# The recurrence scan written out, with key times value as a third rank-one term of VectorE's update

## What is computed

```python
def step(S, inp):
    qt, kt, vt, at, gft = inp
    bs1 = jnp.einsum('bhk,bhkv->bhv', kt, S)
    S1 = S + at[..., :, None] * bs1[..., None, :]
    S2 = jnp.exp(gft)[..., None] * S1
    bs2 = jnp.einsum('bhk,bhkv->bhv', kt, S2)
    S3 = S2 + at[..., :, None] * bs2[..., None, :] + kt[..., :, None] * vt[..., None, :]
    o = jnp.einsum('bhk,bhkv->bhv', qt, S3)
    return (S3, o)
```

## Time and profile before

| what | value |
|---|---|
| median of 3 runs (lowest, highest) | 6515.56 us (6512.77, 6517.51) |
| the profiled execution, its own time | 6517.93 us |
| its span, first to last instruction | 6516.2 us |
| VectorE busy over the span | 3547.5 us (54%) |
| TensorE busy over the span | 5086.6 us (78%) |
| ScalarE, GpSimd busy over the span | 2825.8 us, 1792.3 us |
| VectorE's chief group in the layers, L1878 | idle ahead of it 452.0 us, 441.1 of it until TensorE's L1067 |

### The profile page before, as it was taken

How to read it: one execution, slowest core, us unless ns; L and a number is a source line. 1 busy time by engine, 2 the same in 40 slices (tenths; PEclk the granted TensorE clock), 3 DMA queues, 4 the chain that set the end, 5 groups by cost and what they waited for, 6 DMA issues and landing times. The chain is left out here.

```text
span 6516.2 us, 116951 instructions
## 1 busy us (share of the span) xinstructions
PE 5086.6 (78%) x37588; PEld 3128.5 (48%) x37588; DVE 3547.5 (54%) x15640; ACT 2825.8 (43%) x5416; POOL 1792.3 (28%) x3788
## 2 busy tenths in 40 slices
PE   7998999999999999969989989991000003998999
PEld 5775555555555555557744447760000002444676
DVE  2225666666666666522246631227888886664111
ACT  3334666666666666523335533331000000553333
POOL 1012556555565655510112210000111110221000
PEclk9998999999999999979989979995555555998999
DMA  1000000000000000000010000001000000000000
GB/s 50 1 0 9 2 2 9 2 9 2 9 2 5 6 5 2 1 1 1 0 27 2 2 3 1 0 19 71 0 0 0 0 0 11 2 2 1 1 0 13
DMA packets 36317, 43.85 MB, mean 7 GB/s; under 512 B 15584, under 2 KB 23040, under 8 KB 35456
## 3 DMA queue, kind: packets, MB, share of 16 engines
q1 hardware_dynamic: 35840, 37.74, 1.9%
HBM read 27.64 MB, written 10.09 MB: 6 GB/s over the span
## 5 line engine op out<-in xcount | busy, mean ns | idle before, releaser
L1398 PEld LDWEIGHTS ps<-w,arena 128*128 128x128 f32 x8192 | 1071.4, 192 | 463.0 <-issue 458.9
L1878 DVE CUSTOM_DVE_ANT_0 arena<-ps,mask_win 128x256 f32<-128x256 f32 (+1 forms) x3072 | 1011.2, 386 | 452.0 <-PE ps L1067 441.1
L1728 ACT ACTIVATE arena<-ps,eb 128x512 f32<-128x512 f32 x1024 | 703.6, 687 | 1120.3 <-PE ps L1388 1120.3
L2097 DVE SCALAR_TENSOR_TENSOR X<-ps,C,X 128x128 f32 (+1 forms) x1024 | 289.1, 344 | 1474.1 <-PE ps L1398 1473.1
L1398 PE MATMUL ps<-w,arena 128*128 128x128 f32 x8192 | 1083.6, 275 | 0.0
L1388 PE MATMUL ps<-arena,w 128*128 128x512 f32 x2048 | 1055.2, 598 | 4.6 <-ACT arena L1722 4.6
L1563 ACT ACTIVATE arena<-ps 128x512 f32<-128x512 f32 (+1 forms) x1536 | 754.4, 544 | 598.6 <-PE ps L1077 596.8
L1077 PE MATMUL ps<-arena 32*128 32x512 f32 (+1 forms) x3072 | 873.2, 589 | 16.6 <-ACT arena L1563 10.1
L1067 PE MATMUL ps<-arena 32*128 32x256 f32 (+1 forms) x6144 | 834.0, 381 | 39.8 <-ACT arena L1536 38.6
L1491 PE MATMUL ps<-arena,ones 128*128 128x342 f32 x16 | 9.4, 764 | 967.6 <-DVE arena L2315 964.2
L1067 PEld LDWEIGHTS ps<-arena 32*128 32x128 f32 x6144 | 494.8, 185 | 324.4 <-issue 102.6
(11 more groups left out here) (260 smaller groups left out, 7856.5 us busy)
## 6 DMA issues: line engine op xcount, KB each, us to landing
w<-in_L_w_dram SPq DMA_DIRECT2D x2, 2048.0 KB
scr_k<-arena SPq DMA_DIRECT2D x8, 256.0 KB, 2.1
scr_v<-arena SPq DMA_DIRECT2D x8, 256.0 KB, 2.3
scr_f<-arena SPq DMA_DIRECT2D x8, 256.0 KB, 2.3
arena<-scr_k SPq DMA_DIRECT2D x1, 2048.0 KB, 7.9
arena<-scr_f SPq DMA_DIRECT2D x1, 2048.0 KB, 12.4
arena<-scr_v SPq DMA_DIRECT2D x1, 2048.0 KB, 16.8
out_dram<-X SPq DMA_DIRECT2D x1, 2048.0 KB, 8.7
```

The source lines that it names most:

```text
L1398: m = pe.matmul(ps[:, 2 + (p * E + e) % 2, i * P:(i + 1) * P], hid[c % 2][:, i * P:(i + 1) * P], W2(e)[:, c, :], start=(c == 0 and i == 0) ...
L1728: act.activation(hid[c % 2], ps[:, c % 2, :], gelu, bias=b1(e)[:, c:c + 1])\
L1878: x = dve.tensor_tensor_reduce(out=seen, in0=bank[:, s.at(v):s.at(v) + s.kw], in1=mask, scale=1.0, scalar=NO_SCORE, op0=ALU.add, op1=ALU.m ...
```

## The change

Five things change together:

- The loop over turns of 8 steps becomes 512 steps written out one after the other. All values that are waited for are constants; the register instructions, branches and gates are gone.
- GpSimd's product and the semaphore `kv_ready` are gone. L2292 with them: the decayed state goes straight into column 0 of MJ. In its place the outer product has three terms: k times v, a times w.S, u times k.S.
- MJ has rows of four floats, for three before.
- The four vectors of a step, (w, k, a, u), lie in one array KU, and VectorE reads them from there: the first multiply takes rows 0 and 1, the outer product rows 1 to 3. ScalarE copies the value v beside the two dot products (VXY) and the decay (Fs), and no longer copies KW and UA.
- The loaded keys lie in TMP and their squares in SQ, where they were in UA and TMP.

```diff
-        KW = take(TOKENS, 2, HD)
-        UA = take(TOKENS, 2, HD)
+        KU = take(TOKENS, 4, HD)
...
-        KV = take(STEP_RING, HD, HD)
-        FS = take(HD, HD)
-        MJ = take(HD * HD, 3)
+        MJ = take(HD * HD, 4)
...
-        XY = take(2, HD)
+        VXY = take(STEP_RING, 3, HD)
...
-            with pool.Fori(0, TOKENS // STEP_RING) as it:
...
-                    pool.tensor_tensor(slot, vv, kk, ALU.mult).then_inc(R.kv_ready, 1)
...
-            with act.Fori(0, TOKENS // STEP_RING) as it:
...
-                    act.activation(KWs[:, ring], KW[:, bass.ds(t0, half)], copy)
-                    act.activation(UAs[:, ring], UA[:, bass.ds(t0, half)], copy)
...
+            for h in range(TOKENS // half):
+
+                act.wait_ge(R.step, half * h + 1)
+                times = slice(half * h, half * (h + 1))
+                ring = slice(half * (h % 2), half * (h % 2 + 1))
+                act.activation(VXY[:, ring, 0, :], VD[:, :, times].rearrange("p v t -> p t v"), copy)
+                act.activation(Fs[:, ring], FD[:, :, times].rearrange("p k t -> p t k"), copy)\
+                    .then_inc(R.staged, 1)
...
-            kn, wv, ua, av = KW[:, :, 0, :], KW[:, :, 1, :], UA[:, :, 0, :], UA[:, :, 1, :]
-            chain.link(dve.tensor_tensor(TMP, KD, KD, ALU.mult))
+            wv, kn, av, ua = (KU[:, :, r, :] for r in range(4))
+            chain.link(dve.tensor_tensor(SQ, KD, KD, ALU.mult))
...
+            for t in range(TOKENS):
+                j = t % STEP_RING
+                s = SH[:, (j - 1) % STEP_RING]
+                new = SH[:, j]
+                if t % half == 0:
+                    dve.wait_ge(R.staged, t // half + 1)
+                dve.wait_ge(R.step, t + 1 + half)
+                chain.add(dve.tensor_tensor(
+                    M1.rearrange("p (r v) k -> p r v k", r=2),
+                    s.unsqueeze(1).broadcast_to([P, 2, HD, HD]),
+                    KU[:, t, 0:2, :].unsqueeze(2).broadcast_to([P, 2, HD, HD]), ALU.mult))
+                chain.add(dve.tensor_tensor(
+                    MJ[:, :, 0].rearrange("p (v k) -> p v k", k=HD), s,
+                    Fs[:, j].unsqueeze(1).broadcast_to([P, HD, HD]), ALU.mult))
+                dve.wait_ge(v_chain, chain.value() - 1)
+                chain.link(dve.tensor_reduce(VXY[:, j, 1:3, :].rearrange("p r v -> p (r v)"), M1, AX_X, ALU.add))
+                chain.link(dve.tensor_tensor(
+                    MJ[:, :, 1:4].rearrange("p (v k) r -> p r v k", k=HD),
+                    KU[:, t, 1:4, :].unsqueeze(2).broadcast_to([P, 3, HD, HD]),
+                    VXY[:, j].unsqueeze(3).broadcast_to([P, 3, HD, HD]), ALU.mult))
+                dve.tensor_reduce(new.rearrange("p v k -> p (v k)"), MJ, AX_X, ALU.add).then_inc(R.step, 1)
+                if t >= TOKENS - SEEN and j == STEP_RING - 1:
+
+                    seen = slice(t - (TOKENS - SEEN) - j, t - (TOKENS - SEEN) + 1)
+                    dve.wait_ge(R.step, t + 2 + half)
...
```

More of the change, by code:

```diff
@@ L49 @@
 ROOT_AT = (1, 1)
-PER_TURN = {'dve causal': (26, 2), 'pool causal': (26, 2), 'scan': (40,), 'scan seen': (42,),
+PER_TURN = {'dve causal': (26, 2), 'pool causal': (26, 2),
             'pool moe 2': (52, 4), 'pool moe 1': (26, 2), 'dve moe input': (38, 4),
@@ L335, in __init__ @@
         self.scan_in = sem("r_scan_in")
-        self.kv_ready = sem("r_kv_ready")
         self.staged = sem("r_staged")
@@ L478, in build @@
         GATE = take(BATCHES, OUT)
-        KD = UA.rearrange("p a b c -> p (a b c)")[:, 0:HD * TOKENS].rearrange("p (a b) -> p a b", b=TOKENS)
+        KD = TMP
+        SQ = KU.rearrange("p a b c -> p (a b c)")[:, 0:HD * TOKENS].rearrange("p (a b) -> p a b", b=TOKENS)
         at[0] = 4 * HD * TOKENS + 2 * HD * TOKENS
-        KV = take(STEP_RING, HD, HD)
-        FS = take(HD, HD)
-        MJ = take(HD * HD, 3)
+        MJ = take(HD * HD, 4)
         SH = take(STEP_RING, HD, HD)
         M1 = take(2 * HD, HD)
-        XY = take(2, HD)
+        VXY = take(STEP_RING, 3, HD)
         OQ = take(STEP_RING, HD, HD)
-        KWs = take(STEP_RING, 2, HD)
-        UAs = take(STEP_RING, 2, HD)
         Fs = take(STEP_RING, HD)
@@ L1782, in _ @@
             half = STEP_RING // 2
-            act.wait_ge(R.step, 1)
-            gate(act)
-            with act.Fori(0, TOKENS // STEP_RING) as it:
[L1786 to L1791, removed]
-                    act.activation(KWs[:, ring], KW[:, bass.ds(t0, half)], copy)
-                    act.activation(UAs[:, ring], UA[:, bass.ds(t0, half)], copy)
-                    act.activation(Fs[:, ring], FD[:, :, bass.ds(t0, half)].rearrange("p k t -> p t k"), copy)\
-                        .then_inc(R.staged, 1)
+            for h in range(TOKENS // half):
[5 more added lines that the diff above has]
+                    .then_inc(R.staged, 1)
             barrier(act, PH_REC + 1)
@@ L2247, in _ @@
             over_k = lambda a: a.unsqueeze(1).broadcast_to([P, HD, TOKENS])
-            kn, wv, ua, av = KW[:, :, 0, :], KW[:, :, 1, :], UA[:, :, 0, :], UA[:, :, 1, :]
-            chain.link(dve.tensor_tensor(TMP, KD, KD, ALU.mult))
-            chain.link(dve.tensor_reduce(N2, by_time(TMP), AX_X, ALU.add))
+            wv, kn, av, ua = (KU[:, :, r, :] for r in range(4))
+            chain.link(dve.tensor_tensor(SQ, KD, KD, ALU.mult))
+            chain.link(dve.tensor_reduce(N2, by_time(SQ), AX_X, ALU.add))
             chain.link(dve.tensor_scalar(N2, N2, 1e-24, None, ALU.max))
@@ L2269, in _ @@
             half = STEP_RING // 2
[L2270 to L2309, removed]
@@ new lines, in _ @@
+            for t in range(TOKENS):
[22 more added lines that the diff above has]
+                    dve.wait_ge(R.step, t + 2 + half)
+                    chain.link(dve.tensor_tensor(
+                        OQ, SH, QD[:, :, seen].rearrange("p k t -> p t k").unsqueeze(2)
+                        .broadcast_to([P, STEP_RING, HD, HD]), ALU.mult))
+                    chain.link(dve.tensor_reduce(OD[:, :, seen].rearrange("p v t -> p t v"), OQ, AX_X, ALU.add))
```

## The result

| | before | after |
|---|---|---|
| median (7 runs each) | 6517.51 us | 6537.92 us |
| lowest, highest | 6512.77, 6525.11 | 6534.43, 6541.77 |
| ratio to before, 95% interval | | 1.0032 (1.002 to 1.0044) |
| span of the profiled execution | 6516.2 us | 6535.9 us |

The account below looks back on a forecast made before the run. The scan was taken as a serial VectorE chain; steps 827.4 + closing pairs 39.3 + seams 15.4 = 882.1 us against 863.9, +18.2, less 0.7 for staging: +17.5, median 6533 us, range 6490 to 6560.

Parts of the forecast that it names:

- second multiply to first sum: Scan step: 0.13 us if strided stores don't hold the next instruction, 0.13 + 0.04 if they do; 0.14 taken.
- outer product and gap: Scan step: 192 elements stored every fourth float take 0.46 us, plus 0.035 until the reader starts.
- last sum and gap: End of scan step: sum reads 256 elements for 192, 0.424 us plus 0.035.
- seams, 106: Every fourth scan step: a stand-alone wait ahead of the first multiply adds 0.145 us, 15.4 us in all, bounds 0 and 24.
- closing pairs: Two instructions closing each turn of 8 in the last 176 steps: unchanged, 22 pairs, 39.3 us.
- The deciding step: Outer product: every-fourth-float stores cost more than every third; rival of absent or small surcharge, 6498 or 6476 us, chance 0.22.
- two rules for short instructions: Outer product's lone-store surcharge: 0.6 of the long rows' (0.08 us) or all of it (0.13), giving 0.435 to 0.485.
- outer bound: Outer product's duration: outer bounds 0.36 and 0.485 us around the 0.46 taken.
- The nearest row: Seam price taken from L2257, behind a stand-alone wait: starts 0.18 us late where 0.035 is normal, +0.145.
- fewer instructions: Rival for the scan step: each instruction costs its fixed 0.155 us anywhere, step 1.39, time 6417 us; chance 0.03.
- The instruction fetch: Rival for the scan: written-out VectorE code isn't fetched in time, 20 exposed packets add 23 us, 6556; chance 0.08.
- signs of being wrong: Scan: forecast wrong if the step is under 1.58 us, or if gaps appear that no wait explains.

Follow-up runs that it names:

- innermost run: After with the term index innermost in KU, VXY and M1, so the outer product walks MJ three neighbouring floats at a time: 6475.81 us, 0.9932 of before.
- Before, written out: Before's six-instruction step, GpSimd product and three ScalarE copies kept, loops written out as 512 steps with constant waits: 6472.39 us, 0.993 of before.
- the last run: After, term index innermost, copies' wait on the second multiply, key times value as its own multiply before the outer product, its key staged contiguously by ScalarE: 6436.76 us, 0.9875.
- rows of eight: After with rows of MJ eight floats apart, four of them used: 6543.93 us, 1.0038 of before.
- planes: After with MJ as four planes of 64 floats, stores contiguous and the last sum's reads 256 bytes apart: 6554.67 us, 1.0055 of before.
- the wait moved: Wait for ScalarE's copies moved from first to second multiply: on after 6533.35 us (1.0024 of before), with term index innermost too 6470.52 us (0.9924).

## Why the forecast held, point by point

| term | forecast | measured |
|---|---|---|
| first multiply to second | 0.21 | 0.21 |
| second multiply to first sum | 0.14 (0.13 to 0.17) | 0.13 |
| first sum and gap | 0.312 | 0.31 |
| outer product and gap | 0.495 (0.36 to 0.52) | 0.53 |
| last sum and gap | 0.459 | 0.46 |
| step | 1.616 | 1.64 |
| 512 steps | 827.4 us | 839.7 us |
| seams, 106 | 15.4 us (0 to 24) | 8.0 us |
| closing pairs | 39.3 us | 39.2 us |
| scan | 882.1 us | 887.1 us |

**The deciding step was right.** The forecast said that a store every fourth float costs more than one every third, and with it the change turns from a gain to a loss. The innermost run removes the outer product's surcharge and is at 0.9932 of before, though its set-up is 5 us longer. Had the surcharge been absent, the change would have brought 0.7% or a little more.

**Its size was too small.** I took the middle between two rules for short instructions, 0.46; the full price is what holds: 0.155 + 192 x 1.72 = 0.485. That was my outer bound, and the measured 0.495 lies even above it. The surcharge over contiguous is 0.66 to 0.72 ns an element at 64, 128 and 192 elements (260 or 264 to 218, 376 to 292, 495 to 358). The discount that I carried over from the short rows at every third float doesn't hold at every fourth. This was 18 us too little (0.035 x 512), of which 5 came back in the other terms of the step (its period is 0.024 too low).

**The seams were priced too high,** 0.145 for 0.075, 7 us too much. The nearest row was a bare instruction that waits for two semaphores and increments a third; the one after waits for one. Before, written out, has bare instructions that wait for two and increment none: the gap there is 0.133 us, 0.098 over normal. So the second wait explains 0.02 to 0.03 of the difference of 0.07; whether the increment is the rest wasn't tested. The two errors, of opposite sign, leave 5 us; the 3 us by which the scan started earlier than before, of which the forecast had 0.7, hide about half of that. The forecast is nearer than its terms are, and that is luck.

**The seams of before were read rightly, all but one part.** They are 55 us of idle time over the normal gap (73.0 - 18) and 39 us of stretch. The written-out run gets 43 of the first back and none of the second. The part that I missed lies in the closing pairs: I gave both gaps there the normal 0.035, but in before VectorE idles 0.17 ahead of L2305 and 0.24 ahead of L2307, 9.1 us in all; after has 0.8 ahead of each line. So writing out also brought 7.5 us there, which my sum had among the 103 us of the seams. The 103 themselves are nearer 100: a step of before takes 1.416 us by the median of its 512, where I read 1.41 off one pair of rows.

**Where the new step's 115 us come from** (512 times the difference of the median periods, 1.641 and 1.416), by the runs: 29 from spacing the old 192 elements at four floats in place of three; 61 from 64 more elements in the outer product (0.495 less 0.376), of which 27 are their surcharge (137 ns less 84); 34 from the wider last sum (0.420 less 0.353); less 8 for L2292, whose removal shortens the way from sum to outer product from 0.33 to 0.31. Together 116. That is why the rival "fewer instructions" was out by over 100 us: the instruction that went stood in a slot in which VectorE had to wait anyway, and the last run puts another one there at a gain. The Trainium skill's advice (VectorE: DVE Perf Modes, Rules for kernel authors) to minimise the number of operations doesn't hold in this chain: six instructions at 1.45 us beat five at 1.50.

**The instruction fetch** was no rival. The queue that I had priced has 269 packets in both kernels; the other instruction queue went from 208 (on the page before) to 229. The two on the page after (packets, MB, share of the engines' span):

```profile
q8 instruction: 269, 4.41, 0.3%
q14 instruction: 229, 1.88, 0.1%
```

But gaps that no wait explains did appear, as the forecast's signs of being wrong allowed for: four in 887 us, 0.8 us together. The first multiply at 4607.92 starts 0.35 later than at any other seam (the profile puts this down to ScalarE, whose copy for that half ring had ended at 4601.27), a first sum at 4648.13 starts 0.08 late, and the second multiplies at 5052.60 and 5094.30 start 0.41 and 0.39 after the first in place of 0.21. The kernels with rows of eight, with planes and with the term index innermost have them at the same four steps; the kernels with the wait moved have none. Their cause is open.

## What to carry to other kernels

In a serial chain of short VectorE instructions a float32 operand, read or written, should not stand alone in its 16 bytes in the order in which it is walked (three together cost nothing); reordering the walk (the term index innermost) gained 0.14 us of 1.64 without touching the arithmetic. Count an instruction by what it adds between the end of one result and the start of its reader: one that fits beside a running sum is nearly free, and one removed from there gives almost nothing back (0.016 us a step here). Where two rows of a trace disagree on a price (0.6 or all of a surcharge here) and the sign hangs on it, measure that price by itself first.

## What the runs showed of the chip

- A float32 element stored alone in its 16 bytes costs VectorE 0.64 to 0.72 ns on top of 1.04, in instructions of 64 to 4096 elements; one read alone costs 0.64. The trace before had that price for reads as well: L2250 sums 4096 floats that it reads 512 apart and takes 7.03 us, as the stores of L2254 do. The Trainium skill (Advanced Engine Details and Errata, SBUF Cachelines) has the line length; the runs agree in that rows of four and of eight floats cost nearly the same (495 and 502 ns) while three neighbours in a row of four cost nothing (358).
- At every third float the surcharge is 0.20 to 0.22 ns an element in instructions of 64 and 128, and 0.34 in one of 1368. The long row is another operation (L2325, SCALAR_TENSOR_TENSOR), but that isn't the reason: over 512 contiguous elements it takes 683 ns (L2019) and TENSOR_TENSOR 692 (L2343). No run tells why the two prices differ; what I wrote of long and short instructions isn't borne out at every fourth float.
- Lone stores don't delay the next instruction's start (0.13 after 64 of them), lone reads do (0.17 after 64).
- GpSimd's product blocks whichever two-input multiply it meets until it ends, and lets a sum pass: 0.5 us a meeting, with 0.68 us of work on GpSimd.
- With the term index innermost six set-up multiplies of 4096 elements take 7.4 to 7.6 us, for 4.4 once and 7.1 to 7.2 five times in after; the set-up lasts 81.1 us for 76.2, and these 5 us are inside the 6475.81.
